# Query fills held over: taken out at the head of slots 4 to 8 in a cross-attention and spectral FFN kernel

## The reference

```python
x = x + xattn(layernorm(x), ctx, mask)      # q = xn @ wq + bq, k, v from ctx
#   score = q k^T / sqrt(32) * mask;  score = where(score == 0, -1e9, score)
#   context = softmax(score) @ v;     out = context @ wo + bo
x = x + ffn(layernorm(x))                   # y = real(ifft(fft(x) @ w)) + bias
```

## Time and profile before

| | kernel before |
|---|---|
| median of 3 runs | 458.94 us (458.43 to 459.73) |
| the profiled execution | 458.93 us, of which 457.1 us are the span of the trace |
| TensorE busy | 442.1 us, 97% |
| VectorE busy | 398.0 us, 87% |
| ScalarE busy | 372.6 us, 82% |
| GpSimd busy | 359.6 us, 79% |

### The profile page before, as it was taken

One profiled execution on the slowest core, in us unless ns is written; L12 is line 12 of the kernel. 1 busy time (PEld: TensorE's weight loads), 2 busy tenths in 40 slices (PEclk: granted clock), 3 DMA queues, 4 the chain that ended last, 5 costly groups with the idle time before them and its releaser, 6 DMA issues.

```text
span 457.1 us, 11172 instructions
## 1 busy us (share of the span) xinstructions
PE 442.1 (97%) x3510; PEld 293.3 (64%) x3510; DVE 398.0 (87%) x630; ACT 372.6 (82%) x1434; POOL 359.6 (79%) x540
## 2 busy tenths in 40 slices
PE   6989898999999999999999999999999999999997
PEld 5777686777666666666666666666666666555444
DVE  3797699899999999999999999999999898999443
ACT  3358597789999999898989898989989888899720
POOL 6588744795889899998989898869899685976663
PEclk9999998999999999999999999999999999999999
DMA  8996752332445454545555445445433334330344
GB/s 288 392 368 182 236 195 71 97 86 71 90 92 142 122 147 115 152 110 143 128 134 138 116 107 148 91 114 147 115 96 70 97 74 98 70 93 13 82 104 126
DMA packets 85287, 60.16 MB, mean 132 GB/s; under 512 B 40141, under 2 KB 72813, under 8 KB 84718
## 3 DMA queue, kind: packets, MB, share of 16 engines
q1 hardware_dynamic: 84508, 59.29, 47.3%
q10 hardware_dynamic: 722, 0.17, 0.2%
HBM read 29.33 MB, written 8.39 MB: 83 GB/s over the span
## 4 chain that ended last, share of the span: by engine, by line
PE 79%; DVE 10%; issue 5%; ACT 3%; DMA 1%; ACTq 0%; POOL 0%; DVEq 0%
PE bank L438 32%; PE bank L525 17%; PE bank L582 10%; PE bank L599 6%; PE scores L570 5%; PE bank L443 4%; DVE zs L867 3%; PE bank L595 3%; DVE zs L860 1%; ACT zs L688 1%; DMA bqb<-in_bq 1%; PE scores L443 1%; DVE cn L883 1%; ACT pt L697 1%; DVE x L845 1%
## 5 line engine op out<-in xcount | busy, mean ns | idle before, releaser
L688 ACT ACTIVATE zs<-zs,nbias 128x128 f32<-128x128 f32 x512 | 199.6, 397 | 8.2 <-POOL nbias L1093 7.9
L688 ACT ACTIVATION_READ_ACCUMULATOR zs<-zs,nbias 128x1 f32 x512 | 99.4, 194 | 0.0
L867 DVE SCALAR_TENSOR_TENSOR zs<-zs 128x1024 f32<-128x1024 f32 x64 | 81.3, 1270 | 0.2
L872 DVE TENSOR_REDUCE nmin<-zs 128x8 f32<-128x1024 f32 x64 | 78.1, 1220 | 2.2
L860 DVE TENSOR_TENSOR zs<-scores,ms 128x1024 f32<-128x1024 f32 x64 | 78.0, 1218 | 0.3 <-issue 0.3
L525 PE MATMUL bank<-xth,wqh 128*128 128x256 f16 x256 | 70.9, 277 | 4.0 <-DVE kl L810 2.0
L697 ACT COPY pt<-bank 128x512 f32<-128x512 f32 x128 | 68.4, 586 | 6.7 <-PE bank L582 6.3
L525 PE MATMUL bank<-xtl,wqh 128*128 128x256 f16 x256 | 70.4, 275 | 0.0
L525 PE MATMUL bank<-xth,wql 128*128 128x256 f16 x256 | 70.4, 275 | 0.0
L582 PE MATMUL bank<-ident,zs 128*128 128x128 f32 x512 | 67.5, 275 | 0.7 <-ACT zs L688 0.7
L1053 POOL TENSOR_TENSOR xs<-xs,bob 128x512 f32<-128x512 f32 (+1 forms) x41 | 42.4, 1036 | 24.5 <-DVE zs L867 24.5
(11 more groups left out here) (118 smaller groups left out, 960.1 us busy)
## 6 DMA issues: line engine op xcount, KB each, us to landing
xs<-in_x SPq DMA_DIRECT2D x16, 512.0 KB, 4.2
xtr<-in_xt SPq DMA_DIRECT2D x16, 512.0 KB, 4.4
out<-x SPq DMA_DIRECT2D x31, 256.0 KB, 2.6
qs<-qh SPq DMA_DIRECT2D x120, 64.0 KB
lp<-in_lparts SPq DMA_DIRECT2D x4, 1024.0 KB, 9.0
qs<-ql SPq DMA_DIRECT2D x60, 64.0 KB
ms<-in_mask SPq DMA_DIRECT2D x16, 128.0 KB, 2.6
wqs<-in_wq SPq DMA_DIRECT2D x2, 512.0 KB, 6.8
```

The lines of the kernel that those rows point to most:

```text
L688: last = act.activation(z, z, ACT.Exp, bias=nbias[:, s % 4, i:i + 1], scale=-NEG, accum_out=zsum[:, s % 4, i:i + 1])
L867: dve.scalar_tensor_tensor(out=z, in0=z, scalar=0.0, in1=z, op0=ALU.is_equal, op1=ALU.subtract).then_inc(eq_done, 1)
L872: dve.tensor_reduce(nmin[:, s % 4, :], zs[:, s % NZ].rearrange("p t h k -> p (t h) k"), AX.X, ALU.min).then_inc(mn_done, 1)
```

## The change

In slots 4 to 8 the held fills are moved: `hi` goes to the head of ScalarE's slot, ahead of `copy_rec`; `lo` goes behind `ctx_norm` and ahead of the zero test on VectorE. In all other slots nothing changes, and the mid fills stay where they were.

```diff
@@ ScalarE, head of the slot @@
                 held, mids = slots[v][1:]
+                soon, held = (held, []) if 4 <= v <= 8 else ([], held)
+                for n in soon:
+                    hi(n)
                 if 0 <= v - 4 < NS:
                     copy_rec(v - 4)
@@ VectorE @@
                 if 0 <= v - 4 < NS:
                     ctx_norm(v - 4)
+                soon, held = (held, []) if 4 <= v <= 8 else ([], held)
+                for n in soon:
+                    lo(n)
                 if 0 <= v < NS:
                     zero_to_neg(v)
```

## The result

The changed kernel took 461.93 us (median of 5 runs, 461.33 to 462.82) beside 458.94 us (5 runs, 458.43 to 459.73): a ratio of 1.0063, 95% interval 1.0045 to 1.0082. Forecast was 460.4 us. It is slower as forecast, but by 3.0 us instead of 1.45, just above the range of 458.8 to 461.8. Its profiled execution took 462.15 us, span 460.4. The page gives the first lead: GpSimd has gone from 0% to 4% of the chain that ended last, with 1.2 us more busy time.

What follows compares the result with a forecast made beforehand. TensorE, busy for 97% of the span, was taken as the bound. Its gain turned into +0.65 us, given back later; the low clock's 1.45 us remained: 458.93 + 1.45 = 460.4 us, range 458.8 to 461.8.

Steps and rivals of the forecast that it cites:

- Slot 4: ScalarE's first copy waits for the held fill: `od` at 63.43 instead of 62.05, VectorE's `us` at 63.84, +1.31 us.
- Slots 5 and 6: TensorE's scores idle 1.3 us, the `ql` wait goes, then U2 waits for VectorE's folds until 74.9, +0.65 us.
- The gain of 1.65 us: With the 1.60 us wait for `ql` gone, slot 6's transposes start at 71.26 instead of 72.91.
- The clock: After TensorE's 2.8 us gap ahead of U2 the low clock follows, costing 1.45 us; chance 0.45.
- the ScalarE path: From the stacking's landing through `rec` and `ctx_lo` to WO(0,0): +1.1 us, covered by TensorE's +1.45 at low clock.
- Slot 7: Stacking of chunk 2 lands 1.2 us earlier, about 81.6; `rec` starts at 82.45, WO(0,0) +1.1 us at full clock.
- Behind slot 8: Old order holds; VectorE, about 1 us late entering slot 9, catches up by slot 10; other moved steps cost nothing.
- Rival 1: Clock stays at 2.4 GHz, ScalarE's path decides: 460.0 us, or down to 459.2 with earlier landing; chance 0.25.
- Rival 2: Stacking does not land earlier, staying at 82.8: WO(0,0) +2.3 us, 461.2 us; chance 0.14.
- Rival 3: ScalarE's late start in slot 4 does no harm and the change wins: 457.7 or 457.1 us; chance 0.10.
- Rival 4: The early subtraction still waits for `qh`, so the change doesn't do what it says: about 460.0 us; chance 0.06.

Runs made afterwards that it cites:

- first profile: Profiled execution of the changed kernel's first group of five runs: 462.15 us, group median 461.93 us.
- second profile: Profile of the changed kernel run once more, unaltered, beside later experiments: median 461.58 us, ratio 1.0067.
- The first of the two last versions: Against the original kernel: move only in slots 5 and 6, Q(3,3) ahead of U2, memset of `tb` ahead of bias additions; 458.07 us, ratio 0.9985.
- the three kernels with the 20 matmuls: 20 unused-data matmuls ahead of U2, added to: the changed kernel, 461.24 us; the move in slots 4 to 6, 459.98; the changed kernel with third `srow` buffer, 460.29.

## Why the prediction was right in sign and wrong in size

*Slot 4.* Right. Own times are `od` 63.41 (forecast 63.43), `us` 63.82 (63.84), and the new wait ahead of it is 1.47 us.

*Slots 5 and 6.* Right. The scores are at 68.49, Q(3,1) at 70.03, the transposes at 71.35, U2 at 74.96 (forecast 68.5, 69.95, 71.26, 74.9), own. The gain of 1.65 us came as 1.56 us and went into the folds as written; the kernel with slots 5 to 8 shows the same gap even with VectorE on time.

*The clock.* The level was forecast for the likeliest case and was seen in the first profile, at 1.2 GHz for some three microseconds. From U2 to the transposes of slot 7 it took 7.49 us, against 5.80 in before, so 1.69 us against my 1.45. But the same kernel with the same gap ran the second time at the full level, and the medians of the two groups of five, 461.93 and 461.58, differ by far less than 1.69 us. What the clock costs at the end is about 0.6 us (2.84 against 2.24 own), because the ScalarE path behind it is nearly as late. The mean granted clock on record for each single run says the same: six of the ten have 0.996 and a median of 462.00, four have 1.0 and 461.34 us. The kernel before has both levels too: of its 46 runs beside the experiments nine have 0.996 (median 459.01) and 37 have 0.999 or more (458.52), and the profiled run from which I counted, at 458.93, is one of the nine's kind. At the full clock, then, the change costs 2.8 us, so the low clock is not what the sum lacked. So its chance, 0.45 against 0.25, was too sure of itself, and its price is a maximum of two terms, as I had it, but not the term that mattered.

*Slot 7.* Right at its place. The landing was forecast for 81.6 and read off at 81.92 with the offset (81.58 own); `rec`, forecast at 82.45, is at 82.30 own in the second profile with the full clock, and WO(0,0) at +1.08 against +1.1. The figure of the Trainium skill, page "DMA: Bandwidth & Descriptors", section "Latency and other measured facts", a DMA's fixed cost of about 2 us, which would have given 80.7, an estimate, did not hold here: the last row copies are issued until 79.06 and release `srow` at 81.92, 2.9 us as in before.

*Behind slot 8.* This is the step that failed. I let VectorE's lateness be absorbed by slot 10, because VectorE had 1.4 us of waits for `mh` to give away, and cost `least` and all that follows from it at nothing. I had looked at those who wait on the chain, and for GpSimd at one row only, `ctx_lo`. The minimum of slot 7 was late by 3.7 us: 1.4 us from slot 4, 1.63 us of wait for `rec`, and 0.66 us for the two subtractions ahead of the zero test. It goes to GpSimd's `nbias`, 2.0 us more than WO(0,0) is late itself, and behind that stood work with hardly a gap for 14 us, of which two pieces got 1 us slower each. My terms end at +1.74 us for WO(0,0); what came on top is 0.40 us up to the M piece (of it 0.24 wait for `tb`) and 0.71 us up to slot 10's weighing (of it 0.47 wait for `rzb`). Then 0.28 us is taken back where before had its wait of 0.55 us, and 0.27 us comes on up to 129.45 in small parts, the largest being the projection at 123.10 and the transposes ahead of it, each 0.11 us longer from start to start (2.70 instead of 2.59, 0.98 instead of 0.87). Sum 1.10 us, so 2.84 us. With the start offset of 0.34 us this is the 3.2 us between the two profiled runs.

*The chances.* By its own terms the prediction's chances add up to 0.05 for faster, 0.51 for the same and 0.44 for slower, not 0.06, 0.48 and 0.46.

*The rivals.* Rival 1 occurred in the second profile as far as WO(0,0), and didn't come out at 460.0 because of the same missed term. Rival 2 did not happen: the landing moved with the queue by 1.2 us. Rival 3 fails at its condition, `od` being 1.36 us late. Its kind of gain may exist: without slots 4 and 7 to 8, with the gap filled and `tb` earlier, the kernel is 0.15% faster, but how much of that is the move was not tested. Rival 4 is out by the waits that vanished.

*The cause.* Shown by runs: slot 4's ScalarE wait (+1.5 us alone); slot 7's wait for the landing (4.0 us alone, 0.7 without it); growth behind WO(0,0) of 1.1 to 1.3 us in all six profiles in which `nbias` of slot 7 is 2.0 us later than WO(0,0), none with slots 4 to 6 or slot 4 alone, and almost none where GpSimd's additions were moved forward. The first of the two last versions gives 1.2 us back there without slot 7 as well, since TensorE got ahead of GpSimd's queue (`nbias` of slot 7 is 2.65 us later than before when counted against WO(0,0)). The wait for the landing moves TensorE and GpSimd alike. The growth comes where GpSimd is late against TensorE. Not settled: how the growth divides between the late minimum and the two slower pieces on GpSimd. The two come together: the slow `rzb` copy is in every profile that grows and at that place in none of the others. Not settled either is whether the load of `bqb` lands late by chance: it releases TensorE at 8.83 in both profiles of the changed kernel and between 8.22 and 8.89 in the others, the start-up code being the same in all.

## What to carry to other kernels

A step moved to the head of an in-order queue brings all its waits along. Those on data are looked at first; look as well at the one for a buffer's release, since what is queued behind pays for each. Then follow the delay through every queue that takes it on, in particular an engine that is off the chain but busy for 95% of the next slots, up to the next instruction of TensorE that waits for it. Count that delay against TensorE's own: where both are late by the same amount, nothing more is lost. And where an engine stands idle ahead of a late input, put ready work of its own there (Q(3,3) ahead of U2) before pulling on other engines; work added beside a full VectorE on GpSimd is not free.

## What the hardware did that I had not expected

**GpSimd and VectorE hold each other up.** Three folds (two SBUF operands) took 1.99 us beside GpSimd's instructions on two values a partition, 3.30 and 4.17 us beside its additions, the additions 3.38 to 3.50 instead of 2.50. In the changed kernel itself the zero test of slot 9 meets GpSimd's additions and the `rzb` copy behind them: it takes 2.01 us instead of 1.22, and the copy 1.39 instead of 0.39.

```profile
97.52 2.01 DVE L870 SCALAR_TENSOR_TENSOR zs<-zs 128x1024 f32<-128x1024 f32 x1
```

The Trainium skill, page "SBUF — State Buffer", section "Who interferes with whom", states that VectorE instructions with two SBUF inputs and GpSimd's reads exclude one another; these rows agree: the folds read two parts from SBUF, and the zero test reads `zs` as both of its tensor operands. I had not weighed that rule for work that the change moves side by side.

**The clock.** A gap of 1.60 us brought 1.2 GHz and one of 1.70 us did not the earlier trace rows; 1.59 us did in the kernel with slot 4 alone, and 1.59 and 1.60 us, ahead of the same instruction, did not in the two kernels with slot 7 alone; 2.58 us did in the first profile of the changed kernel and 2.57 us did not in the second, nor 2.58 us with slots 5 to 8. The length of the last gap does not decide it, and one profiled run can't price it. In the three kernels with the 20 matmuls the gap was cut to about 0.35 us, and all 16 runs have a mean clock of 1.0.
